# The passage from the router to the experts: products of the identity between its steps, an exponential ahead of two normalisations, and a shorter reciprocal root

## The reference

```python
logits = xf @ router_w + router_b
probs = softmax(logits); topk_p, topk_i = top_k(probs, 2)
topk_p = topk_p / clip(topk_p.sum(-1), 1e-9)
# every (token, expert) pair gets a rank within its expert, 640 places for each of 8 experts
slot = where(rank < cap, expert * cap + rank, dropped)
h  = gelu(buf[e] @ w1[e] + b1[e])          # 640 x 512 @ 512 x 1024
eo = h @ w2[e] + b2[e]                     # 640 x 1024 @ 1024 x 512
out[token] += eo[slot] * weight            # then x = layernorm(x + out)
```

## Time and profile before

| | |
|---|---|
| median of 3 runs | 1915.85 us (1915.01 to 1916.55) |
| profiled execution: its own time | 1918.52 us |
| its span, first to last instruction | 1916.7 us |
| mean granted clock | 0.987 of 2.4 GHz |
| PE / PEld busy | 1868.9 / 1279.0 us |
| DVE / ACT / POOL busy | 1259.0 / 887.7 / 824.1 us |

### The profile page before, as it was taken

One profiled execution on the slowest core, in us unless ns is written; L12 is line 12 of the kernel. 1 busy time (PEld: TensorE's weight loads), 2 busy tenths in 40 slices (PEclk: granted clock), 3 DMA queues, 4 the chain that ended last, 5 costly groups with the idle time before them and its releaser, 6 DMA issues.

```text
span 1916.7 us, 26614 instructions
## 1 busy us (share of the span) xinstructions
PE 1868.9 (98%) x9972; PEld 1279.0 (67%) x9972; DVE 1259.0 (66%) x2389; ACT 887.7 (46%) x1592; POOL 824.1 (43%) x745
## 2 busy tenths in 40 slices
PE   8999999999999999999999999999969999999996
PEld 6886787788655555555445545544448998889995
DVE  5675564267777788888778778778554444344448
ACT  3312322322666666666556456546724443334431
POOL 4002201100588888888667667665021223321132
PEclk9999999999999999999999999999979999999998
DMA  8003425684668586747543534442244454534453
GB/s 281 23 1 116 161 96 172 210 245 146 153 133 174 108 195 133 168 103 171 132 124 93 128 80 118 113 105 67 77 140 125 132 138 109 143 96 125 128 143 115
DMA packets 124496, 250.10 MB, mean 130 GB/s; under 512 B 11312, under 2 KB 29504, under 8 KB 119680
## 3 DMA queue, kind: packets, MB, share of 16 engines
q1 hardware_dynamic: 108608, 185.46, 32.6%
q0 software_dynamic: 14672, 60.85, 15.5%
q10 hardware_dynamic: 1088, 2.10, 0.3%
HBM read 148.46 MB, written 62.42 MB: 110 GB/s over the span
## 4 chain that ended last, share of the span: by engine, by line
PE 83%; DVE 13%; DMA 1%; issue 1%; ACT 1%; POOL 0%; SPq 0%; POOLq 0%; DVEq 0%; ACTq 0%
PE banks L1192 35%; PE banks L1483 12%; PE banks L1382 11%; PE banks L1352 10%; DVE max L1696 9%; PE banks L1371 9%; PE banks L1403 4%; PE banks L1198 2%; DMA raw<-in_x_t 1%; PE banks L1283 1%; DVE den_c L1715 0%; DMA raw<-in_wk_t 0%; DVE stats_y L1939 0%; PE banks L1360 0%; DVE xg L1923 0%
## 5 line engine op out<-in xcount | busy, mean ns | idle before, releaser
L1696 DVE TENSOR_REDUCE max<-banks 128x1 f32<-128x512 f32 x1024 | 627.8, 680 | 129.5 <-PE banks L1352 128.4
L2208 POOL TENSOR_TENSOR probs<-probs,probs 128x512 f32<-128x512 f32 x464 | 583.3, 1294 | 232.1 <-PE banks L1382 232.1
L2087 ACT ACTIVATE probs<-banks 128x512 f32<-128x512 f32 x1024 | 521.5, 606 | 259.2 <-PE banks L1371 258.5
L1352 PE MATMUL banks<-k_stack,q_stack 98*128 98x512 f32 x1024 | 428.9, 426 | 0.1
L1371 PE MATMUL banks<-q_stack,k_stack 98*128 98x512 f32 x1024 | 377.3, 399 | 2.5 <-ACT probs L2087 2.5
L1352 PEld LDWEIGHTS banks<-k_stack,q_stack 98*128 98x128 f32 x1024 | 192.1, 188 | 191.4 <-DVE max L1696 107.3
L1382 PE MATMUL banks<-probs,v_grp 128*32 128x512 f32 x2048 | 250.1, 600 | 0.0
L1371 PEld LDWEIGHTS banks<-q_stack,k_stack 98*128 98x128 f32 x1024 | 192.3, 189 | 60.3 <-ACT probs L2087 15.9
L2255 POOL DMA_INDIRECT y_rows<-eo,tok x35 | 68.3, 1951 | 171.2 <-DVE eo L1909 112.4
L1896 DVE TENSOR_TENSOR hid_lo<-hid,hid_hi 128x640 fp32r<-128x640 f32 x64 | 52.8, 826 | 133.5 <-ACT hid_hi L2153 133.5
L1382 PEld LDWEIGHTS banks<-probs,v_grp 128*32 128x32 f32 x2048 | 59.9, 109 | 108.1 <-issue 102.0
(11 more groups left out here) (266 smaller groups left out, 2804.1 us busy)
## 6 DMA issues: line engine op xcount, KB each, us to landing
k_stack<-k_parts SPq DMA_DIRECT2D x144, 256.0 KB, 5.4
probs<-probs POOLq DMA_DIRECT2D x36, 1024.0 KB, 10.1
w_raw<-in_L_ffn_w SPq DMA_DIRECT2D x16, 2048.0 KB, 8.6
q_stack<-q_parts SPq DMA_DIRECT2D x48, 256.0 KB
v_grp<-v_rows SPq DMA_DIRECT2D x48, 256.0 KB, 3.4
raw<-in_ctx_t SPq DMA_DIRECT2D x8, 1024.0 KB, 6.8
k_parts<-out_hi SPq DMA_DIRECT2D x32, 256.0 KB, 2.5
k_parts<-out_lo SPq DMA_DIRECT2D x32, 256.0 KB, 3.0
```

The source lines that it names most:

```text
L1352: nc.tensor.matmul(out, queries_of(t)[:, j, tile_of(k)], keys_of(t)[0:STK + SHIFT, j, mc * HALF:(mc + 1) * HALF], start=True, stop=True) \
L1696: V.reduce_max(max4[:, tiles_of(t), :, :][:, k, j, mc:mc + 1], bank(bank_of["max", t, mc, k, j]), AX.X) \
L2087: S.activation(probs_of(t, s)[:, j, :], bank(bank_of["score", t, s, j]), ACT.Exp, scale=SCALE) \
L2208: G.tensor_tensor(a[:, j, :], a[:, j, :], b[:, j, :], ALU.add).then_inc(pair_added.sem, 1)
```

## The change

Three things are edited.

1. PE multiplies the identity by the identity (f32, 128x128 on 128 columns), into bank `NUM`, whose last content has been copied: 22 times after the last half's `logits`, 30 times after its `ranks`, 44 times after its `table`, and 4 times after each of the first four transposed tiles of expert 0. The results are not read. The bank is next used by the first `down`.
2. In the last half's plan two of the four `x2` and `store_x2` are moved behind `logits`, `route_top` and `route_exp`. (The other halves had this order of `x2` and `logits` already.) On ACT this puts the exponential ahead of the x2 of tiles 2 and 3; the stores are asked for after the last x2, as before.
3. The root takes a = (variance + eps) * 0.5 in one instruction, where it took a = variance + eps and, later, a = a * -0.5. The magic constant is made to fit half the variance and to give a negative first value, and each Newton step subtracts 1.5 where it added it, so that each turns the sign; after three steps it is positive. One DVE instruction less in each root, at 8 places with four tiles and at the 5 of `finish`.

```diff
+HALF_MAGIC = RSQRT_MAGIC - 0x400000 - 2 ** 31
+IDLE = {"logits": 22, "ranks": 30, "table": 44, "turn_xe": 4}
@@ plan of the last half
-        for k in range(HT):
+        for k in range(HT // 2):
             do("x2", b, h, k)
-        do("store_x2", b, h)
         do("logits", b, h, ring=next_s_bank)
         do("route_top", b, h)
         do("route_exp", b, h)
+        for k in range(HT // 2, HT):
+            do("x2", b, h, k)
+        do("store_x2", b, h)
         do("route_counts", b, h)
@@ TensorE
+            def idle(stage):
+                pe.wait_ge(*num_copied[LAST])
+                for _ in range(IDLE[stage]):
+                    nc.tensor.matmul(bank(NUM)[:, 0:P], identity[:, :], identity[:, :], start=True, stop=True)
 (in logits and table_sums, at the end)
+                if (b, h) == (B - 1, NH - 1):
+                    idle("logits")                       # idle("table")
 (in ranks, in the branch of the last half)
+                    idle("ranks")
 (in turn_xe, at the end)
+                if e == 0 and i < NS - 1:
+                    idle("turn_xe")
@@ VectorE
-                step.settle(V.scalar_tensor_tensor(y, b, 1.5, y, ALU.add, ALU.mult))
+                step.settle(V.scalar_tensor_tensor(y, b, 1.5, y, ALU.subtract, ALU.mult))
@@ root_begun, and the same in finish
-                step.settle(V.tensor_scalar(a, var, EPS, None, ALU.add))
+                step.settle(V.tensor_scalar(a, var, EPS, 0.5, ALU.add, ALU.mult))
...
-                step.settle(V.tensor_scalar(y.bitcast(I32), y.bitcast(I32), -1.0, float(RSQRT_MAGIC),
+                step.settle(V.tensor_scalar(y.bitcast(I32), y.bitcast(I32), -1.0, float(HALF_MAGIC),
                                             ALU.mult, ALU.add))
-                step.settle(V.tensor_scalar(a, a, -0.5, None, ALU.mult))
```

More of the change, by code:

```diff
@@ L1470, in table_sums @@
                 done.then_inc(table_summed.sem, 1)
+                if (b, h) == (B - 1, NH - 1):
+                    idle("table")
             def turn_xe(e, i):
@@ L1925, in finish @@
                 step.settle(V.bn_aggr(mean_var_s[:, i, :], stats_s[:, i, :]))
-                step.settle(V.tensor_scalar(a, mean_var_s[:, i, 1:2], EPS, None, ALU.add))
+                step.settle(V.tensor_scalar(a, mean_var_s[:, i, 1:2], EPS, 0.5, ALU.add, ALU.mult))
                 step.settle(V.tensor_scalar(y.bitcast(I32), a.bitcast(I32), 1, None, ALU.logical_shift_right))
-                step.settle(V.tensor_scalar(y.bitcast(I32), y.bitcast(I32), -1.0, float(RSQRT_MAGIC),
+                step.settle(V.tensor_scalar(y.bitcast(I32), y.bitcast(I32), -1.0, float(HALF_MAGIC),
                                             ALU.mult, ALU.add))
-                step.settle(V.tensor_scalar(a, a, -0.5, None, ALU.mult))
                 for _ in range(3):
```

## The result

| | before | after |
|---|---|---|
| median of the timed runs, us | 1916.33 (1914.48 to 1919.12, 22 runs) | 1918.82 (1916.67 to 1922.15, 22 runs) |
| ratio | | 1.0014, 95% interval 1.0008 to 1.0019 |
| profiled execution, its span | 1918.52, 1916.7 | 1919.21, 1917.4 |
| mean granted clock | 0.987 | 0.995 |

Slower by 2.5 us. The forecast was +2.8.

A forecast was written before the change was run, and what follows sets the result against it. PE, busy 98% of the span, was taken as the bound, except around the last half's router. +3.96 for the passage, -0.95 tail and -0.2 upstream gave +2.8 us: 1918.7 from the median 1915.85, range 1914.9 to 1921.9.

The forecast's parts named there:

- first up product: Experts' first up product on PE: starts at 1437.50 instead of 1432.18 us, 5.32 us later.
- 12 records now at full clock, start to start: First up products' 12 records: 1.76 us at full clock instead of 3.12 at half clock, -1.36 us.
- whole passage against before: Last half's router passage: +5.32 us from the later up start, -1.36 from the clock, +3.96 us in all.
- tail: Shorter root in the tail: five roots, one DVE instruction of 0.19 us less in each, -0.95 us.
- The price: Identity product on PE: two records of 0.1115 us at full clock, 0.223 us in all.
- The bounds of the price: Identity product on PE: 0.11 us as a transpose to 0.241 with load showing; inner range 0.213 to 0.228.
- Ranks: Ranks' products on PE: start 1.1 us later, but take 1.12 us at full clock, so rt_kp starts at 1414.1 against 1414.09.
- The exponential and the passage's root at nothing: Moved exponential on ACT and passage's root on DVE: covered by the wait for ranks, worth 0; without cover up to 0.6 us.
- The upstream roots: Seven shorter roots before the passage, where PE is through: -0.2 us, bounds 0 and 1.4.
- The blocks fit (first rival): Identity product costs 0.11 us, blocks fit their holes and DVE sets the pace: -4.9 us, 1910.9; chance 0.14.
- The weight load shows (second rival): Identity product costs 0.241 us, blocks overrun by 2.0 us more: 1920.7; chance 0.13.
- The clock falls all the same (third rival): Clock drops to 1.2 GHz near 1411.5 despite the products: up begins +32 us, with roots about 1947; chance 0.03.

The follow-up runs named there:

- e6: The changed kernel with 15, 18, 25 and 3 products (none after the fourth turn), on 8 columns instead of 128: +8.9 us against before.
- e2: The kernel before with only the 112 identity products added, same counts as the change: +3.1 us against before.
- r12: The changed kernel with identity transposes for products and ACT's old order of x2 and exponential, repeated on a third chip: -5.8 us against before.
- r9: The changed kernel with identity transposes for products, same counts 22, 30, 44, 4, repeated on a third chip: -6.6 us against before.
- e1: The changed kernel with all identity products removed, leaving the shorter root and moved exponential: -0.9 us against before.
- e4: The changed kernel with each identity product made a transpose of the identity, same counts 22, 30, 44, 4: -6.4 us against before.
- e3: The changed kernel with identity products cut to 15, 18, 25 and 3, none after the fourth turn: -5.0 us against before.
- e5: The changed kernel with identity transposes only after the table (44) and the turns (4 each), none after logits and ranks: +0.9 us against before.
- e8: The changed kernel with identity transposes, none after the fourth turn, and one DVE split of w1 moved behind the tokens: -3.1 us against before.
- r10: The changed kernel with transposes, none after the fourth turn, and the w1 split behind the tokens, repeated on a third chip: -4.1 us against before.
- e7: The changed kernel with identity transposes for products and ACT's old order of x2 and exponential: -4.2 us against before.

## Why the prediction was right

The forecast held: +2.5 us where +2.8 stood, slower by less than the 0.2%. The mechanism is what the runs bear out, not the last tenths: the interval of the medians is +1.5 to +3.6, and the traces have +3.11 up to the last scatter, so that 2.5 lies so near to 2.8 is in part luck. Step by step, from the logits' first record:

| step | forecast | after |
|---|---|---|
| one product, records x step | 2 x 0.1115 | 2 x 0.112 |
| ranks start | 5.80 | 5.88 |
| rt_kp starts | 7.13 | 7.19 |
| table's products start | 13.61 | 13.69 |
| first turn | 25.20 | 25.31 |
| first up product | 30.53 | 30.55 |
| 12 records now at full clock, start to start | 1.76 | 1.84 |
| whole passage against before | +3.96 | +4.06 |
| tail | -0.95 | -0.95 |
| roots upstream | -0.2 | not shown |

- *The price.* Right, and it is the number that the forecast rested on. It came from the row of k_half and v_half, an f32 product of nearly the same shape, and from counting its records against the products that the code issues. The passage's +4.06 is the shift from the logits to ACT's table load, 32.63 before and 36.69 after; it is also 5.34 - (3.12 - 1.84), the two terms of the forecast's sum.
- *The bounds of the price.* Weaker than the price. 0.241 and 0.213 were worked out from column steps, while a record costs 0.111 us at 8 columns too (e6), so no run shows that the columns set it. And the prediction's inner range, 1917.0 to 1920.4 with a fifth beyond +3.8, doesn't come out of its own terms: with products of 0.213 to 0.228 and the upstream roots between 1.4 and 0 they give +0.5 to +3.6, 1916.3 to 1919.4, and nothing beyond +3.8. The chance of "slower" was too high by that. The measured time lies in both.
- *Ranks.* Right that the full clock pays just there for the overrun: the ranks start 1.2 us later and rt_kp only 0.07.
- *The exponential and the passage's root at nothing.* Right for this change, by e2. The price "without that cover" was up to 0.6; r12 against r9 has 0.35 at rt_kp and 0.28 at the last scatter for the exponential.
- *The upstream roots.* Not shown. If they were worth something, the kernels with the shorter root would have gained more outside the stretch from the logits to the scatter than e2, which has the old one. The median's change less the stretch's is -0.9 us in e2 and between -0.3 (e1) and -2.0 (e4) in the others, after's being -0.6. Nothing stands out of that scatter. The 2.4 us by which after's logits come earlier than before's in the profiles are no proof: e2's come 4.5 earlier.
- *The blocks fit (first rival).* False for the change, since a product is two records. But e4 is that rival made real, with one record of 0.110 us, and it goes as the rival said: rt_kp -1.24 forecast, -1.25 in r9; the table's add -2.0 forecast, -2.14 in r9; in all -4.9 forecast and -4.71 in r9's trace. Its median fell further, by 6.4 and 6.6 us; the 1.9 to 2.0 us beyond the trace are not explained by any stretch that I can name.
- *The weight load shows (second rival).* False: the step in the blocks was 0.112 to 0.114 us, under the 0.116 at which it would decide.
- *The clock falls all the same (third rival).* False: 1.00 in every window. e6 shows that it was no empty fear: with 8 columns PE was through just the same and the clock fell.

The Trainium skill, "TensorE: Matmul & The Clock Gate", Part 4: PE-mode transpose, says that the full clock doesn't engage for transpose mode, which doesn't count as busy in the same way. By that e4 would have gone as before or worse. The rows of e4 above, and r9's 1.00 over the same passage, contradict it for f32 transposes of 128x128 on this chip, and so does e5, where the clock rose inside a block made of nothing else. The measurement decides.

## What to carry to other kernels

Work that is put on an engine only to keep its clock is paid for in the order of that engine's queue: count the records that one such product becomes, measure their step in a near row of the trace, and size each block below the hole ahead of the next instruction that has to be served, leaving the end of the hole empty. Here the kernel with all three edits was 2.5 us slower with 112 products and 5.0 us faster with 67 (e3); one record per product, as a transpose has, gained most (e4). An early block that seems to cover nothing can be what lets the late ones run at full clock at all (e5). And work that is moved off one engine's path can hold up another: DVE's split, moved behind the tokens, lengthened POOL's issue of the gather (e8).

## What the runs showed of the hardware that was not expected

- A stream of f32 products on 8 columns, PE through for 28.5 us, ran at 0.50; the same stream on 128 columns ran at 1.00 (e6, e3). At full clock both cost 0.11 us a record.
- f32 transposes alone held the clock at 1.00 for 11 us (e4) and were what PE ran when it rose from 0.50 (e5).
- An indirect DMA that POOL began to issue during one of DVE's w_lo splits took longer by nearly all that was left of the split: 2.05 us instead of 1.10 (e8, r10), and the same in 31 issues of the kernel before.
- In e5, e7 and e8, measured together on one chip, some of the turns' signals reached ACT late: its first instruction on such a tile started 2.06 to 2.49 us after the turn in e7 and e8 and up to 3.4 in e5, against 0.63 to 0.70 elsewhere at full clock; in e7 the idle time is put down to no engine of the core (its line below). The repeats of e7 and e8 on another chip have none of it, and are 1.6 and 1.0 us faster against before. So it isn't these two kernels' own (e5 was not repeated); its cause stays open.

```profile
1427.11 0.60 ACT L2140 ACTIVATE xe_hi<-banks 128x512 fp32r<-128x512 f32 x1 [2.31 <-remote]
```
